# Eight gather slots in a scores pass, and step words read once in an attention pass

## What is computed

```
score[e, h]  = sum_d q[src[e], h, d] * k[dst[e], h, d]
prob[e, h]   = exp((score[e, h] - max over the edges of dst[e]) / 8)
sums[n, h]   = sum over e with dst[e] == n of prob[e, h] * v[src[e], h]      (and of prob itself)
```

## Time and profile before

| | us |
|---|---|
| median of 3 runs (4047.67 to 4053.07) | 4048.72 |
| the profiled execution, its own time | 4048.99 |
| its span, first to last instruction | 4047.3 |
| scores stage, steps of its loop on VectorE | 192.55 to 810.80 |
| attention stage, loads and loop | 860.9 to 1214 |

### The profile page before, as it was taken

How to read it: one execution, slowest core, us unless ns; L and a number is a source line. 1 busy time by engine, 2 the same in 40 slices (tenths; PEclk the granted TensorE clock), 3 DMA queues, 4 the chain that set the end, 5 groups by cost and what they waited for, 6 DMA issues and landing times. The chain is left out here.

```text
span 4047.3 us, 64299 instructions
## 1 busy us (share of the span) xinstructions
PE 3103.2 (77%) x12404; PEld 2300.5 (57%) x12405; DVE 2122.8 (52%) x3755; ACT 1177.5 (29%) x2663; POOL 1118.4 (28%) x1227
## 2 busy tenths in 40 slices
PE   4767667736666734999998899999996868666979
PEld 2634434424445433567776788888885656554568
DVE  6466666666663286111113455555556874884231
ACT  1000000036662411233333000000007975653312
POOL 2166666601110000000000355555550001750023
PEclk9866665569998875799999999999998989887979
DMA  1588888835550000000000565556650000004134
GB/s 54 174 268 268 267 265 266 268 87 161 160 151 6 18 0 17 0 16 8 16 8 3 173 176 175 174 178 178 175 175 33 0 19 1 1 0 163 78 128 139
DMA packets 219248, 449.64 MB, mean 111 GB/s; under 512 B 30122, under 2 KB 109299, under 8 KB 217771
## 3 DMA queue, kind: packets, MB, share of 16 engines
q1 hardware_dynamic: 158762, 257.80, 20.7%
q0 software_dynamic: 60416, 190.96, 15.9%
HBM read 360.37 MB, written 89.26 MB: 111 GB/s over the span
## 5 line engine op out<-in xcount | busy, mean ns | idle before, releaser
L1401 POOL DMA_INDIRECT conv_h<-table_h,conv_ix x424 | 409.0, 965 | 1048.4 <-ACT conv_ix L1392 957.8
L1452 PE MATMUL bank<-conv_w,conv_eT 128*128 128x256 f32 x2532 | 580.9, 379 | 0.0
L489 PE MATMUL bank<-scores_k,scores_hotT 128*128 x848 | 391.1, 609 | 183.1 <-DVE scores_hotT L518 177.0
L1452 PEld LDWEIGHTS bank<-conv_w,conv_eT 128*128 128x128 f32 x2532 | 482.1, 190 | 64.5
L467 POOL DMA_INDIRECT scores_qv<-table_qv,scores_ix x424 | 400.9, 946 | 374.0 <-ACT scores_ix L457 160.8
L489 PEld LDWEIGHTS bank<-scores_k,scores_hotT 128*128 128x128 f32 x848 | 225.6, 294 | 331.2 <-issue 299.0
L1351 DVE SCALAR_TENSOR_TENSOR x<-bank,soft_w,x 128x256 f32 x200 | 96.8, 484 | 443.2 <-PE bank L1285 443.2
L863 PE MATMUL bank<-attend_pv,attend_hot 128*128 128x260 f32 x848 | 237.2, 403 | 118.9 <-POOL attend_pv L806 83.0
L1313 ACT ACTIVATE soft_h<-bank,soft_bi,soft_sc 128x320 f32<-128x320 f32 x320 | 197.5, 617 | 340.0 <-PE bank L1278 340.0
L1392 ACT ACTIVATE conv_ix<-src 128x2 int32 x212 | 43.2, 204 | 770.1 <-DVE conv_msg L1426 736.6
L863 PEld LDWEIGHTS bank<-attend_pv,attend_hot 128*128 128x128 f32 x848 | 145.2, 190 | 210.8 <-POOL attend_pv L806 121.9
(11 more groups left out here) (420 smaller groups left out, 5250.8 us busy)
## 6 DMA issues: line engine op xcount, KB each, us to landing
conv_eT<-in_edges SPq DMA_DIRECT2D x212, 384.0 KB, 3.3
edge_v<-scores_qv SPq DMA_DIRECT2D x212, 256.0 KB, 4.2
attend_v<-edge_v SPq DMA_DIRECT2D x212, 256.0 KB, 2.7
hidden_rows<-rows SPq DMA_DIRECT2D x25, 512.0 KB, 3.8
top_wd<-in_top_wd SPq DMA_DIRECT2D x8, 1024.0 KB, 11.4
scores_qv<-table_qv,scores_ix POOLq DMA_INDIRECT x424, 4.8
conv_h<-table_h,conv_ix POOLq DMA_INDIRECT x424, 3.3
table_qv<-qkv_rows SPq DMA_DIRECT2D x50, 128.0 KB, 1.7
```

What stands on the lines that cost most here:

```text
L489: mm = nc.tensor.matmul(banks[u][:, g * F:(g + 1) * F], hotT[:, u, g * P:(g + 1) * P], k[:, bass.ds(t, 1), :].rearrange("p t f -> p (t f)" ...
L1401: nc.gpsimd.indirect_dma_start(out=h[:, u, g, :], out_offset=None, in_=m.d_h, in_offset=bass.IndirectOffsetOnAxis(ap=ix[:, u * G + g:u * G ...
L1452: mm = nc.tensor.matmul(banks[u][:, g * F:(g + 1) * F], eT[:, u, g, c], w[:, c], start=c == 0, stop=c == EC - 1)
```

## The change

In the scores stage the ring gets RING = 8 slots. All loops of the stage run over rounds of 8 steps, which makes 27 rounds, or 216 steps, out of 53 rounds of 4. The hot, PSUM and edge_v buffers stay at four, taken modulo 4. Six of the eight slots lie in the SBUF space of x, two in a tensor of their own. Since slots u and u + 4 now store to the same edge_v tensor, SyncE waits, before it issues a store, until the store of four steps ago has landed. The attention stage loads x again from DRAM, ahead of its loads of values on the same queue (3200 KB).

In the attention stage ACT and VectorE read each step's word once, and carry it in registers. ACT reads it between the two Abs. VectorE reads the word of step s + 3 behind weigh(s + 2) and ahead of keep(s), and carries three words from round to round, with three register moves at a round's end.

The diff, cut to its core; all `r * UN + u` of the scores stage become `r * RING + u`, and slot-wise `[u]` of hotT and banks become `[u % UN]`:

```diff
-STEPS = NT * -(-ET // G) + UN
+RING = 8
+STEPS = (NT * -(-ET // G) // RING + 2) * RING
...
-                for k in range(2):
-                    c(nc.vector.tensor_scalar(m.rounds[:, k:k + 1], ends[:, NT - 1:NT], float(UN - 1 - k * UN), None, ALU.add))
-                c(nc.vector.tensor_scalar(m.rounds[:], m.rounds[:], 2, None, ALU.arith_shift_right))
+                for k, many in enumerate((UN, RING)):
+                    for j in range(2):
+                        c(nc.vector.tensor_scalar(m.rounds[:, 2 * k + j:2 * k + j + 1], ends[:, NT - 1:NT],
+                                                  float(many - 1 - j * many), None, ALU.add))
+                    c(nc.vector.tensor_scalar(m.rounds[:, 2 * k:2 * k + 2], m.rounds[:, 2 * k:2 * k + 2], many.bit_length() - 1, None, ALU.arith_shift_right))
...
+def word_at(eng, m, s):
+
+    return eng.value_load(m.steps[0:1, bass.ds(s, 1)])
+
...
-        ix = st.sb("ix", [P, UN * G], I32)
-        qv = st.sb("qv", [P, UN, G, 2 * F])
+        ix = st.sb("ix", [P, RING * G], I32)
+        in_x = NT * F // (G * 2 * F)
+        qv_x = m.x[:].rearrange("p t f -> p (t f)")[:, 0:in_x * G * 2 * F].rearrange("p (u g f) -> p u g f", u=in_x, g=G)
+        qv_more = st.sb("qv", [P, RING - in_x, G, 2 * F])
         hotT = st.sb("hotT", [P, UN, G * P])
...
+        gathered = [st.gather_sem(f"gathered{g}") for g in range(RING * G)]
...
+        def qv(u):
+            return qv_x[:, u] if u < in_x else qv_more[:, u - in_x]
...
+                rounds = rounds_of(sp, m, RING)
...
-                for u in range(UN):
+                        if u < UN:
+                            sp.wait_ge(stored[u + UN], r * 16 + 16)
+                        else:
+                            sp.wait_ge(stored[u - UN], r * 16 + 32)
+                        sp.sem_inc(seen, 1)
+                        sp.dma_start(m.d_v[u % UN][:, bass.ds(i, G), :], qv(u)[:, :, F:2 * F]).then_inc(stored[u], 16)
...
+                act.sem_inc(freed, RING)
...
+                    pe.wait_ge(hots, r * RING + (u + 1 + UN))
+                    pe.wait_ge(freed, r * RING + (u + 1 + RING - UN))
...
+                sp.dma_start(m.x[:], a["x"].rearrange("(t p) f -> p t f", p=P)).then_inc(x_loaded, 16)
...
+                sp.wait_ge(x_loaded, 16)
...
-                def distance(r, u):
-                    t, i = step_at(act, m, r * UN + u)
-                    act.wait_ge(hots, r * UN + (u + 1))
-                    for g in range(G):
-                        nc.scalar.activation(far[:, u, g * P:(g + 1) * P], m.node_no[:, bass.ds(t * P, P)], ACT.Abs,
-                                             bias=minus[:, bass.ds(i + g, 1)]).then_inc(own, 1)
+                def distance(word, u, g):
+                    t, i = node_tile(act, word), edge_tile(act, word)
+                    nc.scalar.activation(far[:, u, g * P:(g + 1) * P], m.node_no[:, bass.ds(t * P, P)], ACT.Abs,
+                                         bias=minus[:, bass.ds(i + g, 1)]).then_inc(own, 1)
...
+                def round_of(r, word, more):
+
+                    for u in range(UN):
+                        if more or u + 1 < UN:
+                            act.wait_ge(hots, r * UN + (u + 2))
+                            distance(word, (u + 1) % UN, 0)
+                            later = word_at(act, m, r * UN + (u + 2)) if more or u + 2 < UN else word
+                            distance(word, (u + 1) % UN, 1)
+                            word = later
+                        one_hot(r, u)
+                    return word
                 last = last_round(act, m)
...
+                def weigh(r, u, word):
+                    i = edge_tile(dve, word)
...
+                def keep(r, u, word):
+                    t = node_tile(dve, word)
...
+                def round_of(r, words, more):
+
                     for u in range(UN):
                         if u + 2 < UN:
+                            weigh(r, u + 2, words[u + 2])
+                        elif more:
+                            weigh(r + 1, u + 2 - UN, words[u + 2])
+                        if more or u + 3 < UN:
+                            words.append(word_at(dve, m, r * UN + (u + 3)))
+                        keep(r, u, words[u])
+                    return words[UN:]
...
+                carried = [dve.alloc_register(f"attend_word{k}") for k in range(3)]
+                for k in range(3):
+                    word = word_at(dve, m, k)
+                    dve.reg_mov(carried[k], word)
...
+                with dve.Fori(0, last) as r:
+                    for x, word in zip(carried, round_of(r, [dve.snap(x) for x in carried], True)):
+                        dve.reg_mov(x, word)
+                round_of(last, [dve.snap(x) for x in carried], False)
```

More of the change, by code:

```diff
@@ L401, in step_at, with node_tile, edge_tile, last_round @@
     return t, i
-def last_round(eng, m):
-    return eng.value_load(m.rounds[0:1, 1:2], min_val=1, max_val=STEPS // UN - 1)
-def rounds_of(eng, m):
-    return eng.value_load(m.rounds[0:1, 0:1], min_val=NT // UN, max_val=STEPS // UN)
+def word_at(eng, m, s):
+    return eng.value_load(m.steps[0:1, bass.ds(s, 1)])
+def node_tile(eng, v):
+    return eng.snap(eng.bass.s_assert_within(v >> PACK, 0, NT - 1,
+                                             skip_runtime_bounds_check_because="the steps are made of tiles that exist"))
+def edge_tile(eng, v):
+    return eng.snap(eng.bass.s_assert_within(v & ((1 << PACK) - 1), 0, ET - G,
+                                             skip_runtime_bounds_check_because="the steps are made of tiles that exist"))
+def last_round(eng, m, many=UN):
+    at = 3 if many == RING else 1
+    return eng.value_load(m.rounds[0:1, at:at + 1], min_val=1, max_val=STEPS // many - 1)
+def rounds_of(eng, m, many=UN):
+    at = 2 if many == RING else 0
+    return eng.value_load(m.rounds[0:1, at:at + 1], min_val=NT // many, max_val=STEPS // many)
 def edge_scores(nc, a, m, banks):
@@ L450, in _ @@
             def _(act):
[L451 to L454 removed]
+                act.sem_inc(freed, RING)
+                with act.Fori(0, rounds_of(act, m, RING)) as r:
+                    for u in range(RING):
+                        s = act.snap(r * RING + u)
                         t, i = step_at(act, m, s)
@@ L460, in _ @@
             def _(pool):
-                with pool.Fori(0, rounds_of(pool, m)) as r:
-                    for u in range(UN):
-                        pool.wait_ge(index, r * UN + (u + 1))
+                with pool.Fori(0, rounds_of(pool, m, RING)) as r:
+                    for u in range(RING):
+                        pool.wait_ge(index, r * RING + (u + 1))
                         pool.wait_ge(stored[u], r * 16 + 16)
@@ L841, in _ @@
-                with dve.Fori(0, last) as r:
+                def round_of(r, words, more):
                     for u in range(UN):
                         if u + 2 < UN:
-                            weigh(r, u + 2)
-                        else:
-                            weigh(r + 1, u + 2 - UN)
-                        keep(r, u)
-                for u in range(UN):
-                    if u + 2 < UN:
-                        weigh(last, u + 2)
-                    keep(last, u)
+                            weigh(r, u + 2, words[u + 2])
[5 more added lines that the diff above has]
+                    return words[UN:]
```

128 lines of the change are left out of this document (55 added, 73 removed).

## The result

The changed kernel takes 3903.0 us (median of 4 runs, 3902.2 to 3905.7), the kernel before 4048.2 (4 runs, 4047.6 to 4053.1): ratio 0.964, 95% interval 0.962 to 0.966. The profiled execution has a span of 3900.5 us, 146.8 under that of before.

What follows compares the result with a forecast made beforehand. Four ring slots' latency was taken to pace the scores stage, VectorE's sequencer attention. Scores -63.0, attention -46, x +6.5, constants +0.6 make -101.9 from 4048.99: 3947 us, with an 8-in-10 range of 3914 to 3997.

Steps and rivals of the forecast that it cites:

- The ring: Scores stage: four slots pace it by latency, a slot's cycle of 11.7 us being 4 x 2.93; eight remove that.
- The step: Scores stage: a step takes 2.55 us, GpSimd's 2.50 plus 0.05 for engines near each other; range 2.46 to 2.75.
- the bound becomes GpSimd's 2.50: Scores stage: with eight slots GpSimd's two gathers of 1.25 us set the step, with VectorE right under it.
- its lower end: Scores step of 2.46 us, VectorE's own, since GpSimd enters with eight slots full and 216 x 0.04 us use less.
- The start: Scores stage: gathers at 205 GB/s leave 173 of 378 GB/s to the key table's load, +4.5 us (0 to 6).
- Attention, 46: Attention loop on VectorE: a round falls from 6.54 to 5.67 us, 0.87 times 53, saving 46 us (20 to 62).
- From 858 to 868: Attention round, lines 822 to 832 before the change: keeps its read and waits, 0.78 us four times, 3.12.
- they cannot fall below 832 itself, 0.43 and a gap: Attention round, line 832 to next 822: at least 0.45 us each; 0.45, 0.55, 0.45, together 1.45, and 1.10 at the jump.
- The named rival with the smaller price for register work (5.37): Attention round of 5.37 us if the four remaining reads take no address, saving 62 us; with step 2.46, chance 0.07.
- x, 6.5: Attention's start: x loads ahead of values on SyncE's queue, moving VectorE's first product from 866.49 to 873, +6.5 us.
- The jumps: Rival, scores loop: doubled bodies fetch code again at each of 27 jumps; 4069 to 4174 us, chance 0.04.
- both better: Rival: scores step 2.46 us and attention round 5.37 us, total 3912 us, chance 0.07.

Runs made afterwards that it cites:

- one wait put back: The changed kernel, but GpSimd's gather also waits until the store of four steps earlier has landed: 3990.5 us, where the kernel before took 4054.0.
- The kernel with the ring alone: The changed kernel's scores pass (eight slots, x loaded again) with the attention loop of the kernel before: 3974.0 us, where the kernel before took 4054.0.
- the kernel with x early: The changed kernel with x's second load moved one stage earlier, between scores and attention: 4166.1 us, where the kernel before took 4227.2.

## Why the forecast was too small

**The ring.** Right, and shown by one wait put back: the cycle of the earlier trace rows, 11.7 us in four slots. SyncE's new wait cost nothing, as said: every store was issued 0.36 to 0.69 us after its gathers had landed, and the store of four steps ago had landed at least 1.7 us before its issue. VectorE's idle time before its product is under 0.2 us a step, DMA share 0.96, 309 GB/s.

**The step, 2.55 for 2.47 (17 us).** The step of the argument that failed is "the bound becomes GpSimd's 2.50". The prediction's own reading had VectorE at 2.46, and 2.47 came. GpSimd is slower than that, but starts ahead: the second gather of a step is issued 21.0 us before its product at the first step and 10.4 us before it at the last, never less, and lands in 5.2 in the median. The lead of eight slots, filled while the key table loads, is spent at 0.05 us a step and is not used up until the last steps, when gathers land late: the last took 10.3 us, and its product waited 0.30 for it. The forecast said this for its lower end, "216 x 0.04 us use up less than that", and then took the other figure with an addition for crowding. Reads of the table did not stretch further: 0.458 us in the mean, 0.460 before. The kernel with the ring alone, whose scores loop has the same code, took 2.505 us a step, again without a product that waited for a gather, so a few hundredths of a us are not resolved here.

**The start, 4.5 for 1.2 (3.3 us).** The key table landed 17.3 us after its issue instead of 16.4. The failed step is that the gathers' 205 GB/s would be missing from the table's load; they delayed it by 0.9 us, and 0.3 more came behind it.

**Attention, 46 for 69.7 (24 us).** From 858 to 868 the forecast had 3.12 us a round, and 3.13 came. The failed step is "they cannot fall below 832 itself, 0.43 and a gap". The add lasts 0.43 us in the record, but the next operation starts 0.34 us after its start: records of neighbours overlap. It could be seen in the earlier trace rows, where two products of 0.69 take 1.29 together. That is 0.34 + 0.34 + 0.41 for 0.45 + 0.45 + 0.55, and 0.99 for 1.10 at the jump: 0.47 a round, 53 times 25 us. The named rival with the smaller price for register work (5.37) lay on the right side and was still too dear. By its own words it isn't 5.37: four addresses of 0.11 taken from 5.67 are 5.23. That this is near 5.21 would have been luck, since 858 to 868 kept its 3.13; what went was between 868 and 858.

**x, 6.5 for 5.8.** Right in size and cause: the kernel with x early takes the wait away. The Trainium skill's "DMA: Bandwidth & Descriptors", Queues, rings and completion order, says that an engine takes the descriptors of one ring in order, and the trace agrees: x, issued at 772.25, landed at 784.08, and the first values, issued at 774.15, at 784.75. The row of x (KB, us from issue to landing):

```profile
x<-in_x SPq DMA_DIRECT2D x1, 3200.0 KB, 11.8
```

**The end of the scores stage, 0 for 3.8.** The stage between scores and attention ended 3.8 us sooner, which the forecast didn't have; all four kernels with the new scores pass on the first chips show it. The stage is left when every engine is done, GpSimd's last instruction (DRAIN) included. Before and after (ns, and the time of its start):

```profile
L431 POOLq DRAIN  x1: 10544/10544/10544, 803.5 to 803.5; - x1
```
```profile
L456 POOLq DRAIN  x1: 18452/18452/18452, 708.3 to 708.3; - x1
```

It ended at 814.05 us before, 9.7 us after GpSimd's last gather was issued and 3.2 us after VectorE's last operation; the next stage's first load went out at 814.29. In the changed kernel GpSimd is ahead, its DRAIN ended at 726.76, and the next load followed VectorE's end (727.35) at 727.89. That is 3.0 of the 3.8 us. All three traces with four slots have the load behind the DRAIN, and all with eight have it behind VectorE; this was read from them, not tried. So GpSimd's lead pays at the end of the stage as well.

**The jumps.** The rival that a larger body fetches its code again is out for 141 instructions of VectorE: between 200 and 700 us one packet of instructions was loaded, and the idle time ahead of a round's first product is 0.69 us in the median, against 0.64 before. The rule of the Trainium skill, "Runtime: NRT & Kernel Launch", Instruction fetch mechanics, wasn't put to work by these loops; no run here shows a jump that fetched.

**The range.** Misses of 17, 3, 24, 1 and 4 us all had one sign, 49 together; for the step, the start and the round the dearer of two readings was taken. 4 came back in the rest of the program. The case "both better" was there with 3912 and a chance of 0.07. And the forecast is for the chips of its trace alone: on the one later chip where the changed kernel itself was timed the change brings 1.5%, which no row of that trace could tell.

## What to carry to other kernels

Where two engines stand near each other, ask which one starts ahead: a lead, filled before the loop, lasts as many steps as the slower one's deficit a step goes into it, and until it is spent the other sets the pace. Here it was some 16 us (21.0 less 5.2 for landing) at 0.05 a step, an estimated 300 steps for a loop of 216. Where a profile says "issue" before every operation, count what the engine's sequencer does in a step (reads, address arithmetic, waits) and remove some; moving a read behind a longer operation gained nothing here, where the sequencer has no hole. Take the smallest distance between two operations from starts to starts, not from durations.

## What the runs showed of the hardware

- A gather of 128 rows costs GpSimd 1.25 us from issue to issue, with rows of 1 KB as with 2 KB.
- VectorE started an operation 0.34 us after the start of one recorded at 0.43 us, and 0.61 us after one of 0.69 (1101.18 to 1101.79).
- GpSimd's DRAIN at the end of the scores stage ended 9.7 us after its last gather was issued, in all three traces with four slots, and the next stage began behind it.
- Chips differ: on three of those met, 0.7 us register instructions come in bunches every 14 us (four steps, eight gathers) on three engines at once, and the scores loop ends 127 us later in the kernel before and 225 in the changed one. They came with two gathers a step, whatever the bytes and the number of slots, and in the one run with one gather a step they didn't. Their cause is open: whether the eight gathers or the 14 us set them wasn't tried apart. What follows attention's loop is some 50 us longer there, which wasn't followed.
